# Keys of a pair of edge tiles turned into one PSUM bank, aggregates in three banks: a graph layer and an expert layer on Trainium2

## The chip, the cores and the metric

The kernel runs on one core of a Trainium2 chip. The metric is the device time of one execution in microseconds; for the kernel before it is the median of three runs. A profile of one further execution goes with it. The engines are called PE (TensorE, the matmuls; PEld are its weight loads), DVE (VectorE), ACT (ScalarE), POOL or GpSimd, and SP (SyncE, which issues DMAs here).

## What is computed

The input is a graph of 3125 nodes with 256 features, 50,000 edges (source, target, type), and weights. There are three message-passing layers, a small perceptron on their result, and a layer of 8 experts of which each node uses two. The change lies in the edge part of the message passing, which is, cut to what matters:

```
Q = (h @ Wq.T + bq).reshape(-1, H, DH)          # H = 4 heads, DH = 64
K = (h @ Wk.T + bk).reshape(-1, H, DH)
V = (h @ Wv.T + bv).reshape(-1, H, DH)
scores = einsum('ehd,egd->ehg', Q[src], K[tgt]) / sqrt(DH)   # per edge, head against head
attn = softmax(scores, axis=-1)
msg = einsum('ehg,egd->ehd', attn, V[tgt]).reshape(-1, HID)
msg = msg + Ee[et]
return segment_sum(msg @ Wo.T + bo, src, num_segments=n_nodes)
```

All of it is in float32. The three layers are followed by `adjustment = relu(hidden @ W1.T + b1) @ W2.T + b2`, and the expert layer takes the top two of 8 experts by a softmax over `x @ Wr + br`.

## The kernel before

The program is written engine by engine, with semaphores set and awaited by hand. It first sorts the edges by source: the nodes are cut into windows of 16 nodes (W), and each tile of 128 edges holds edges of one window only. That gives 294 pairs of edge tiles per layer. A layer is then an edge phase (the function `e_phase`, present once on each engine) and a node phase (`uq_phase`, at the end `uf_phase`). The change touches the edge phase alone. There are three edge phases of 294 pairs, 882 pairs in all.

An edge phase goes through the pairs in 24 full turns of 12 pairs and a last one of 6; the turns between the first and the last are a hardware loop, so a turn's code is written out for 12 pairs. Per pair:

- GpSimd gathers the rows of keys and values (2 KB each) of the targets, one indirect DMA of 128 rows per tile, two per pair (line 574). They go into `kv`, a ring of 24 tiles, so the gathers for a pair start when the aggregates of the pair 12 places earlier are done (the wait on `agg_done` ahead of them).
- PE turns the keys, four transposes of 128 x 128 per pair (`key`, line 1544), into PSUM bank 3 or 4 by turns, and ACT copies that bank to `kt_s` (`keys`, line 1307), which has two buffers.
- ACT also lays the queries of the two windows into a block-diagonal operand (`queries`, lines 1302 and 1303).
- PE multiplies: two masks (`mask`, line 1548) set to a large negative number what doesn't belong to an edge's node, and eight instructions add the scores (`scores`, line 1574), in bank 0, 1 or 2.
- DVE takes the maximum over the 16 nodes, which picks an edge's own scores (`best`, line 829). Every four pairs it does the softmax with ACT's exponential, and per pair it spreads the weights over the window's nodes (`spread`, line 858).
- PE forms the aggregates, the weighted sum of values by node, with eight instructions (`aggregate`, line 1584), in bank 6 or 7 by turns. ACT copies them to `stage`, a ring of three, in two instructions (`sums_out`, line 1314), and DVE adds them to the window's sum (`add`, line 876).

The order of each engine's work is written out by hand. In step p, PE turns the keys of pair p + 1, with the masks of pair p between them (`keys_masks`), then makes the aggregates of pair p - 6 (LAG is 6), then the scores of pair p. ACT copies the keys of p, lays the queries of p + 1, and copies the sums of p - 7. DVE takes the maximum of p, spreads the weights of p - 4, and adds the sums of p - 7.

PE's waits in a step are these: before the keys and masks, for the maximum of pair p - 3 (its score bank is then free) and for the gathers of pair p + 1; before the aggregates, for the spread weights of p - 6 and for the staged sums of p - 8 (the aggregates' bank is then free, `staged` counts them and begins at 8); before the scores, for ACT's copy of the keys of p (`kT_ready`). Bank 5 holds DVE's small softmax results in an edge phase. The semaphores count on over turns and layers; `at[p]` is the count that is reached with pair p of the turn. Before the first layer's loop the counts of some semaphores are raised, so that the first waits pass.

Of the kernel before, what the change touches and what calls it, by code (L numbers as in the profile page):

```python
# [22 lines left out]
P = 128  # L23
N, D, H, DH, E, L = 3125, 256, 4, 64, 50000, 3
# [17 lines left out]
UB = 4  # L42
TURN = 6
EB = -(-(E + -(-N // W) * (P - 1)) // (P * UB))
EP = 2 * EB
# [4 lines left out]
PAIRS = TILES // 2  # L50
HT = TILES // 2
LASTP = 2 * LASTB
HALVES = 2 * NTURN - 1
LAG = 6
# [32 lines left out]
def build(nc, A, out):  # L87
    ctx = ExitStack()
    with ctx:
# [17 lines left out]
        ident = sb("ident", [P, P])  # L107
# [16 lines left out]
        kv = arena[:, 0:n_kv].rearrange("p (b u n) -> p b u n", b=TURN, u=UB)  # L124
# [33 lines left out]
        kt_s = sb("kt_s", [P, 2, 2, KC, P])  # L158
# [156 lines left out]
        bank = [ctx.enter_context(nc.psum_tensor(f"bank{i}", [P, 512], F32)) for i in range(8)]  # L315
# [16 lines left out]
        S = namedtuple("Semaphores", names)(*[sem(n) for n in names])  # L332
# [44 lines left out]

        def u_bank(l, n):
            return bank[n % (4 if l < L - 1 else 3)]

        block = ctx.enter_context(nc.Block())

# [843 lines left out]
        def _(act):  # L1226

            for c in range(NCH):
                b = c % 2
# [64 lines left out]
            def e_phase(l):  # L1294
                def indices(i, h):
                    act.activation(gidx[:, h, :], rec[:, ds(i * TILES + h * HT, HT)], ACT.Copy).then_inc(S.idx_ready, 1)

                def queries(p):
                    for u in range(2):
                        w = act.snap(areg[2 * p + u], min_val=0, max_val=NW - 1)  # L1300
                        q = qt[:, ds(w, 1), :].squeeze(1)
                        act.activation(qbd[0:DH, p % 4, u, 0:64], q, ACT.Copy)  # L1302
                        act.activation(qbd[DH:P, p % 4, u, 64:128], q, ACT.Copy)  # L1303

                def keys(p, at):
                    act.wait_ge(S.kT_done, at[p])
                    act.activation(kt_s[:, p % 2], bank[3 + p % 2][:, :].rearrange("p (u c n) -> p u c n", u=2, n=P),  # L1307
                                   ACT.Copy).then_inc(S.kT_ready, 1)

                def sums_out(p, done, added):  # L1310
                    act.wait_ge(S.agg_done, done)
                    act.wait_ge(S.chain_b, added)
                    for r in range(2):
                        ins = act.activation(  # L1314
                            stage[r * DH:(r + 1) * DH, p % 3].rearrange("p u (h s) -> p u h s", h=H),
                            bank[6 + p % 2][r * DH:(r + 1) * DH, 0:2 * P].rearrange("p (u g s h) -> p g u h s", u=2, g=2, h=H)[:, r],
                            ACT.Copy)
                    ins.then_inc(S.staged, 1)

                def exps(n, ready):  # L1320
                    act.wait_ge(S.exp_in, ready)
                    act.activation(ex[:, 0:2 * n], sx[:, 0:2 * n], ACT.Exp).then_inc(S.exp_out, 1)

                def turn(i, first, last, before_last=False):
                    pairs = LASTP if last else PAIRS
                    at = [act.snap(l * EP + i * PAIRS + p + 1) for p in range(2 * PAIRS - AL)]
                    before = None if first else act.snap(l * EP + i * PAIRS)
                    for p in range(pairs):
                        keys(p, at)
                        if p + 1 < pairs:  # L1330
                            queries(p + 1)
                        elif not last:
                            act.load(areg, wid[0:1, ds((i + 1) * TILES, TILES)])
                            queries(0)
                        if p >= AL or not first:
                            sums_out((p - AL) % PAIRS, at[p + PAIRS - AL], at[p - 1] if p else before)
                        if p % GP == 1 and (p > 1 or not first):
                            exps(GP, act.snap(l * EG + i * GT + p // GP))
                        if p == PAIRS // 2 - 1 and not last:
                            indices(i + 1, 0)  # L1340
                        if p == PAIRS - 1 and not before_last:
                            indices(i + 1, 1)

                for h in range(2):
                    indices(0, h)
                act.load(areg, wid[0:1, 0:TILES])
                queries(0)
                turn(0, True, False)
                with nc.scalar.Fori(1, NTURN - 2) as i:
                    turn(i, False, False)  # L1350
                turn(NTURN - 2, False, False, True)
                turn(NTURN - 1, False, True)
                exps(LASTP - GP * (GL - 1), act.snap(l * EG + EG))
                for p in range(AL):
                    sums_out((LASTP - AL + p) % PAIRS, act.snap(l * EP + EP + p + PAIRS - AL + 1), act.snap(l * EP + EP + p))
# [100 lines left out]
        def _(pe):  # L1456
# [83 lines left out]
            def e_phase(l):  # L1540
                def key(p, u, c):
                    t = 2 * p + u
                    o = u * D + c * P
                    return pe.transpose(bank[3 + p % 2][:, o:o + P], kv[:, t // UB, t % UB, c * P:(c + 1) * P], ident[:, :])  # L1544

                def mask(p, u):
                    m = 2 * (p % 4) + u
# [4 lines left out]
                def keys_masks(k, landed, p, at, here):  # L1552
                    if p is not None:
                        pe.wait_ge(S.score_read, at[p + 1])
                        if p % 4 == 0:
                            pe.wait_ge(oh_landed[p // 4], here[p // 4 // 2])
                    for u in range(2):
                        if k is not None:
                            pe.wait_ge(gathered[2 * k + u], landed)
                        for c in range(KC):  # L1560
                            if k is not None:
                                ins = key(k, u, c)
                            if u == 0 and p is not None:
                                mask(p, c)
                    if k is not None:
                        ins.then_inc(S.kT_done, 1)

                def scores(p, at):
                    bk = bank[p % 3]
                    pe.wait_ge(S.kT_ready, at[p])  # L1570
                    for u in range(2):
                        for c in range(KC):
                            o = u * D + c * P
                            ins = mm(bk[:, o:o + P], kt_s[:, p % 2, u, c, :], qbd[:, p % 4, u, :],  # L1574
                                     start=False, stop=(c == KC - 1), skip_group_check=True)
                    ins.then_inc(S.score_done, 1)

                def aggregate(p, ready):
                    pe.wait_ge(S.att_ready, ready)
                    pe.wait_ge(S.staged, ready)  # L1580
                    for t in (2 * p, 2 * p + 1):
                        b, u, o = t // UB, t % UB, t % 2 * P
                        for g in range(0, H, 2):
                            ins = mm(bank[6 + p % 2][:, o:o + P], kv[:, b, u, D + g * DH:D + (g + 2) * DH],  # L1584
                                     att[:, b % 2, u, :, g:g + 2, :].rearrange("p s g h -> p g s h"),
                                     start=(g == 0), stop=(g == H - 2), skip_group_check=True)
                    ins.then_inc(S.agg_done, 1)

                def turn(i, first, last):
                    pairs = LASTP if last else PAIRS  # L1590
                    at = [pe.snap(l * EP + i * PAIRS + p + 1) for p in range(pairs + 1)]
                    here = [pe.snap((l * (NTURN - h) + i + 1) * 16) for h in range(2)]
                    ahead = pe.snap((l * NTURN + i + 2) * 16)
                    for p in range(pairs):
                        if p + 1 < pairs:
                            keys_masks(p + 1, here[(p + 1) * 2 // PAIRS], p, at, here)
                        elif not last:
                            keys_masks(0, ahead, p, at, here)
                        else:
                            keys_masks(None, None, p, at, here)  # L1600
                        if p >= LAG or not first:
                            aggregate((p - LAG) % PAIRS, at[p])
                        scores(p, at)

                keys_masks(0, pe.snap((l * NTURN + 1) * 16), None, None, None)
                turn(0, True, False)
# [1 line left out]
                    turn(i, False, False)  # L1608
                turn(NTURN - 1, False, True)
                for p in range(LAG):  # L1610
                    aggregate((LASTP - LAG + p) % PAIRS, pe.snap(l * EP + EP + p + 1))

            def update(l, n, ring):
                dst, at = u_bank(l, n), l * NT + n + 1
# [291 lines left out]
```

## Time and profile before

| | |
|---|---|
| three runs, us | 4463.02, 4485.4, 4497.68 |
| median, us | 4485.4 |
| the profiled execution, us | 4478.05 |
| its span, us | 4476.2 |
| mean granted PE clock over the span | 0.918 |
| PE, PEld, DVE, ACT, POOL busy, share of the span | 81%, 71%, 55%, 60%, 53% |

The span is what the trace covers: from the first instruction to the last. Times in a trace are microseconds from its start, those marked ns apart. Busy time doesn't count register, branch, semaphore and DMA-issuing instructions. PE's matmuls are pipelined and their ends are modelled, so that a matmul's bar reaches past the start of the next. Where an engine sat idle, the trace names what ended the wait, as far as the semaphores show it; "remote" is a releaser that it can't name and "issue" is no wait that it can see. A part of the matmul records can be missing.

### The profile page before, as it was taken

Reading aid. Unit: us, or ns where it says so; the run is one execution under the profiler, and the core shown is the slowest. Engines: PE = TensorE matmul, PEld = TensorE weight load, DVE = VectorE, ACT = ScalarE, POOL = GpSimd, SP = SyncE. Lnnn points to the kernel's source line nnn. Section 1 sums busy time; section 2 is a strip of 40 time slices with the busy share of each in tenths; the row PEclk is TensorE's granted clock in tenths of the full one; section 3 lists DMA queues with packets and bytes.
Section 4 is the critical chain, followed back from the end, with each engine's and each line's share of the span. In section 5 each row is a group of like instructions: output and inputs, shape, how many; then the busy total and the mean of one; then the engine's idle time right before and its main releaser. Section 6 shows DMA issues by size and latency. Waiting matters only on the chain.

```text
span 4476.2 us, 90208 instructions
## 1 busy us (share of the span) xinstructions
PE 3636.6 (81%) x26290; PEld 3156.6 (71%) x26291; DVE 2448.8 (55%) x6794; ACT 2699.9 (60%) x8426; POOL 2356.7 (53%) x2552
## 2 busy tenths in 40 slices
PE   6777868887888887788878888878888888887999
PEld 2333547787777775777777777577777777767998
DVE  6555635565656664566566566455566565682111
ACT  4666766666666655666666665566666666543443
POOL 3555324555555565555555555545555555563444
PEclk9777888999999999999999999889999999898999
DMA  2000154555555534555555553445555555445665
GB/s 66 0 0 0 40 198 136 157 165 161 161 162 160 164 116 159 145 165 163 163 165 162 160 162 110 153 141 160 160 164 164 160 158 159 142 158 181 179 186 126
DMA packets 264904, 630.76 MB, mean 141 GB/s; under 512 B 56095, under 2 KB 128726, under 8 KB 256471
## 3 DMA queue, kind: packets, MB, share of 16 engines
q0 software_dynamic: 161376, 477.59, 38.4%
q1 hardware_dynamic: 103431, 152.05, 10.1%
q8 instruction: 40, 0.66, 0.1%
q14 instruction: 57, 0.47, 0.0%
HBM read 577.72 MB, written 52.04 MB: 141 GB/s over the span
## 4 chain that ended last, share of the span: by engine, by line
PE 56%; DVE 14%; issue 12%; another core or an unknown queue 10%; ACT 5%; DVEq 2%; DMA 1%; ACTq 0%; POOL 0%; SPq 0%; POOLq 0%
PE bank L1584 13%; PE bank L1574 12%; PE bank L1777 5%; PE bank L1544 4%; PE bank L1789 4%; DVE att L858 4%; PE bank L1530 3%; PE bank L1548 2%; PE bank L1482 2%; DVE arena L876 2%; DVE sc L829 2%; PE bank L1496 2%; PE bank L1490 2%; PE bank L1524 2%
## 5 line engine op out<-in xcount | busy, mean ns | idle before, releaser
L574 POOL DMA_INDIRECT arena<-kv_d,gidx x1764 | 1672.3, 948 | 1492.4 <-PE bank L1584 514.9
L1584 PE MATMUL bank<-att,arena 128*128 128x128 f32 x7056 | 1023.5, 291 | 494.4 <-DVE att L858 391.2
L1584 PEld LDWEIGHTS bank<-att,arena 128*128 128x128 f32 x7056 | 909.3, 202 | 583.0 <-DVE att L858 468.3
L829 DVE TENSOR_REDUCE sc<-bank 128x32 f32<-128x512 f32 x882 | 606.5, 688 | 948.9 <-remote 513.6
L1574 PE MATMUL bank<-qbd,kt_s 128*128 128x128 f32 x7056 | 1014.8, 290 | 67.0 <-issue 34.2
L1307 ACT ACTIVATE kt_s<-bank 128x512 f32<-128x512 f32 x882 | 526.6, 597 | 870.1 <-PE bank L1544 552.9
L1574 PEld LDWEIGHTS bank<-qbd,kt_s 128*128 128x128 f32 x7056 | 933.3, 205 | 78.4 <-issue 40.4
L1544 PE MATMUL bank<-ident,arena 128*128 128x128 f32 x3528 | 766.0, 283 | 51.1 <-issue 25.7
L858 DVE TENSOR_TENSOR att<-bank,oh 128x512 f32<-128x512 f32 x882 | 602.1, 683 | 26.4 <-PE bank L1584 0.4
L1314 ACT ACTIVATE stage<-bank 64x128 f32<-64x128 f32 x1764 | 478.4, 271 | 164.5 <-PE bank L1584 118.6
L1544 PEld LDWEIGHTS bank<-ident,arena 128*128 128x128 f32 x3528 | 493.7, 148 | 82.3 <-issue 54.0
L876 DVE TENSOR_TENSOR arena<-stage,arena 128x64 f32 x1764 | 400.6, 227 | 196.1 <-issue 94.5
L1302 ACT ACTIVATE qbd<-arena 64x64 f32 x1764 | 441.5, 250 | 50.7 <-issue 40.4
L1303 ACT ACTIVATE qbd<-arena 64x64 f32 x1764 | 449.2, 255 | 20.5
L1548 PE MATMUL bank<-maskc,oh 128*128 128x256 bf16 x1764 | 453.5, 282 | 4.2 <-issue 4.2
L558 POOL DMA_INDIRECT rec_d<-arena x241 | 245.1, 1017 | 257.7 <-DVE arena L770 186.4
L756 DVE CUSTOM_DVE_ANT_0 arena<-bank,arena 128x200 f32<-128x200 f32 x391 | 138.8, 364 | 193.7 <-PE bank L1496 102.7
L1214 DVE TENSOR_TENSOR arena<-bank,arena 128x256 f32<-128x256 f32 x56 | 23.8, 425 | 356.6 <-PE bank L1789 356.6
L1234 ACT ACTIVATE arena<-arena 128x592 bf16<-128x592 f32 x150 | 105.2, 776 | 181.5 <-DVE arena L773 177.3
L1490 PE MATMUL bank<-arena 128*128 128x200 bf16 x391 | 114.5, 305 | 118.4 <-DVE rank L756 77.3
L1777 PE MATMUL bank<-xT,arena 128*128 128x128 f32 x1792 | 210.5, 276 | 0.1
L1777 PEld LDWEIGHTS bank<-xT,arena 128*128 128x128 f32 x1792 | 205.7, 193 | 0.5 <-ACT xT L1437 0.5
(246 smaller groups left out, 4211.8 us busy)
## 6 DMA issues: line engine op xcount, KB each, us to landing
arena<-in_pack SPq DMA_DIRECT2D x56, 1030.0 KB
arena<-kv_d,gidx POOLq DMA_INDIRECT x1764
oh<-oh_d SPq DMA_DIRECT2D x222, 64.0 KB
kv_d<-arena SPq DMA_DIRECT2D x50, 256.0 KB, 2.0
xin<-hid_d SPq DMA_DIRECT2D x75, 128.0 KB
arena<-in_w SPq DMA_DIRECT2D x8, 1024.0 KB, 8.3
kv_d<-arena SPq DMA_DIRECT2D x5, 1280.0 KB, 5.1
hid_d<-arena SPq DMA_DIRECT2D x50, 128.0 KB, 2.0
```

Of the source, the lines that this page charges most:

```text
L574: pool.indirect_dma_start(kv[:, t // UB, t % UB, :], None, kv_d, bass.IndirectOffsetOnAxis(gidx[:, h, t - h * HT:t - h * HT + 1], 0),).the ...
L829: dve.tensor_reduce(sc[:, 2 * m:2 * m + 2], bank[q % 3][:, :].rearrange("p (t g s h) -> p t g h s", t=2, g=H, s=W), AX.X, ALU.max).then_in ...
L858: dve.tensor_tensor(att[:, b, u:u + 2].rearrange("p t s g h -> p t s (g h)"), at_s[:, 2 * m:2 * m + 2].rearrange("p t g h -> p t (g h)").u ...
L876: dve.tensor_tensor(a, stage[:, p % 3, u, :], a, ALU.add).then_inc(S.chain_a if u == 0 else S.chain_b, 1)
L1303: act.activation(qbd[DH:P, p % 4, u, 64:128], q, ACT.Copy)
L1307: act.activation(kt_s[:, p % 2], bank[3 + p % 2][:, :].rearrange("p (u c n) -> p u c n", u=2, n=P), ACT.Copy).then_inc(S.kT_ready, 1)
L1314: ins = act.activation(stage[r * DH:(r + 1) * DH, p % 3].rearrange("p u (h s) -> p u h s", h=H), bank[6 + p % 2][r * DH:(r + 1) * DH, 0:2 ...
L1544: return pe.transpose(bank[3 + p % 2][:, o:o + P], kv[:, t // UB, t % UB, c * P:(c + 1) * P], ident[:, :])
L1548: mm(bank[p % 3][:, u * D:(u + 1) * D], oh[:, p // 4, 1, :], maskc[:, m:m + 1, :].to_broadcast([P, H, DH]), start=(u == 0), stop=False, sk ...
L1574: ins = mm(bk[:, o:o + P], kt_s[:, p % 2, u, c, :], qbd[:, p % 4, u, :], start=False, stop=(c == KC - 1), skip_group_check=True)
L1584: ins = mm(bank[6 + p % 2][:, o:o + P], kv[:, b, u, D + g * DH:D + (g + 2) * DH], att[:, b % 2, u, :, g:g + 2, :].rearrange("p s g h -> p ...
L1777: ins = mm(bank[1 + 2 * (p % 2) + h // 4][:, (h % 4) * P:(h % 4 + 1) * P], w1s[:, p, c * HID + h * P:c * HID + (h + 1) * P], xT[:, p % 2, ...
```

## The change

The keys of a pair are turned into bank 3 alone, and the aggregates go round three banks, 4, 6 and 7. So PE must have ACT's copy of the keys of pair p before it turns those of pair p + 1, and the wait on `kT_ready` moves from the scores to the head of the step; only the last step of a phase, which turns no keys, keeps it at the scores. The aggregates of pair p - 6 then need the staged sums of p - 9 in place of p - 8, so their wait on `staged` is for one less; a register `before` holds that count for the first pair of a turn.

```diff
+        def sum_bank(p):
+            return bank[(4, 6, 7)[p % 3]]
...
-                    act.activation(kt_s[:, p % 2], bank[3 + p % 2][:, :].rearrange("p (u c n) -> p u c n", u=2, n=P),
+                    act.activation(kt_s[:, p % 2], bank[3][:, :].rearrange("p (u c n) -> p u c n", u=2, n=P),
...
-                            bank[6 + p % 2][r * DH:(r + 1) * DH, 0:2 * P].rearrange("p (u g s h) -> p g u h s", u=2, g=2, h=H)[:, r],
+                            sum_bank(p)[r * DH:(r + 1) * DH, 0:2 * P].rearrange("p (u g s h) -> p g u h s", u=2, g=2, h=H)[:, r],
...
-                    return pe.transpose(bank[3 + p % 2][:, o:o + P], kv[:, t // UB, t % UB, c * P:(c + 1) * P], ident[:, :])
+                    return pe.transpose(bank[3][:, o:o + P], kv[:, t // UB, t % UB, c * P:(c + 1) * P], ident[:, :])
...
                         if p % 4 == 0:
                             pe.wait_ge(oh_landed[p // 4], here[p // 4 // 2])
+                    if k is not None and p is not None:
+                        pe.wait_ge(S.kT_ready, at[p])
...
-                def scores(p, at):
+                def scores(p, at, last):
                     bk = bank[p % 3]
-                    pe.wait_ge(S.kT_ready, at[p])
+                    if last:
+                        pe.wait_ge(S.kT_ready, at[p])
...
-                def aggregate(p, ready):
+                def aggregate(p, ready, emptied):
                     pe.wait_ge(S.att_ready, ready)
-                    pe.wait_ge(S.staged, ready)
+                    pe.wait_ge(S.staged, emptied)
...
-                            ins = mm(bank[6 + p % 2][:, o:o + P], kv[:, b, u, D + g * DH:D + (g + 2) * DH],
+                            ins = mm(sum_bank(p)[:, o:o + P], kv[:, b, u, D + g * DH:D + (g + 2) * DH],
...
+                    before = None if first else pe.snap(l * EP + i * PAIRS)
...
-                            aggregate((p - LAG) % PAIRS, at[p])
-                        scores(p, at)
+                            aggregate((p - LAG) % PAIRS, at[p], at[p - 1] if p else before)
+                        scores(p, at, last and p + 1 == pairs)
...
-                    aggregate((LASTP - LAG + p) % PAIRS, pe.snap(l * EP + EP + p + 1))
+                    aggregate((LASTP - LAG + p) % PAIRS, pe.snap(l * EP + EP + p + 1), pe.snap(l * EP + EP + p))
```

## Rows read from the trace of the kernel before

**Rows 1.** Table by stretch; busy us of PE, PEld, DVE, ACT, POOL; PEclk

```profile
645.00:1653.00 1008.00, 810.12 (x6466) 767.01 (x6467) 603.11 (x1542) 633.61 (x2174) 563.66 (x604) 0.93 0.55 159
...
sum 3022.00, PE 2429.77 PEld 2301.01 DVE 1784.51 ACT 1900.87 POOL 1690.48; mean PE 809.92 PEld 767.00 DVE 594.84 ACT 633.62 POOL 563.49
```

**Rows 2.** Groups by line; columns: busy us, mean ns, idle before, releasers

```profile
L574 POOL DMA_INDIRECT arena<-kv_d,gidx x1764 | 1672.3, 948 | 1492.4 <-PE bank L1584 514.9 <-issue 488.9 <-remote 352.6
...
L1584 PE MATMUL bank<-att,arena 128*128 128x128 f32 x7056 | 1023.5, 291 | 494.4 <-DVE att L858 391.2 <-issue 91.8 <-ACT stage L1314 9.3
...
L1574 PE MATMUL bank<-qbd,kt_s 128*128 128x128 f32 x7056 | 1014.8, 290 | 67.0 <-issue 34.2 <-ACT kt_s L1307 32.0
...
L829 DVE TENSOR_REDUCE sc<-bank 128x32 f32<-128x512 f32 x882 | 606.5, 688 | 948.9 <-remote 513.6 <-PE bank L1574 404.9 <-issue 28.9
...
L1307 ACT ACTIVATE kt_s<-bank 128x512 f32<-128x512 f32 x882 | 526.6, 597 | 870.1 <-PE bank L1544 552.9 <-remote 259.8 <-issue 45.4
```

**Rows 3.** Waits: us in total, times, longest

```profile
PE bank L1574 <- ACT kt_s L1307: 32.0, 14, 17.1
```

**Rows 4.** Timeline of GpSimd: start, duration, gather, idle before

```profile
948.54 0.94 POOL L574 DMA_INDIRECT arena<-kv_d,gidx  x1 [1.85 <-PE bank L1584]
...
954.79 0.95 POOL L574 DMA_INDIRECT arena<-kv_d,gidx  x1 [0.30 <-issue]
...
958.16 0.94 POOL L574 DMA_INDIRECT arena<-kv_d,gidx  x1 [2.43 <-remote]
...
961.46 0.94 POOL L574 DMA_INDIRECT arena<-kv_d,gidx  x1 [1.10 <-PE bank L1584]
...
968.22 0.95 POOL L574 DMA_INDIRECT arena<-kv_d,gidx  x1 [1.39 <-PE bank L1584]
...
974.73 0.95 POOL L574 DMA_INDIRECT arena<-kv_d,gidx  x1 [1.82 <-PE bank L1584]
```

**Rows 5.** Timeline of a held stretch

```profile
951.55 0.38 PE L1544 MATMUL bank<-ident,arena 128*128 128x128 f32 x2
...
953.91 1.06 PE L1574 MATMUL bank<-qbd,kt_s 128*128 128x128 f32 x8
...
954.69 0.14 PEld L1544 LDWEIGHTS bank<-ident,arena 128*128 128x128 f32 x1
...
957.25 0.69 DVE L829 TENSOR_REDUCE sc<-bank 128x32 f32<-128x512 f32 x1 [3.86 <-remote]
...
957.32 0.60 ACT L1307 ACTIVATE kt_s<-bank 128x512 f32<-128x512 f32 x1 [4.39 <-PE bank L1544]
...
958.59 2.08 PE L1584 MATMUL bank<-att,arena 128*128 128x128 f32 x8 [1.86 <-DVE att L858]
```

**Rows 6.** Timeline of quiet steps

```profile
945.00 0.60 ACT L1307 ACTIVATE kt_s<-bank 128x512 f32<-128x512 f32 x1
...
945.31 0.14 PEld L1544 LDWEIGHTS bank<-ident,arena 128*128 128x128 f32 x1
...
945.97 0.97 PEld L1584 LDWEIGHTS bank<-att,arena 128*128 128x128 f32 x8
...
961.96 0.15 PEld L1544 LDWEIGHTS bank<-ident,arena 128*128 128x128 f32 x1
...
962.50 0.38 PE L1544 MATMUL bank<-ident,arena 128*128 128x128 f32 x2
...
962.62 0.97 PEld L1584 LDWEIGHTS bank<-att,arena 128*128 128x128 f32 x8
...
962.92 0.60 ACT L1307 ACTIVATE kt_s<-bank 128x512 f32<-128x512 f32 x1 [1.37 <-PE bank L1544]
...
963.51 0.97 PEld L1574 LDWEIGHTS bank<-qbd,kt_s 128*128 128x128 f32 x8
...
964.40 0.14 PEld L1544 LDWEIGHTS bank<-ident,arena 128*128 128x128 f32 x1
```

**Rows 7.** Table by stretch, after the held stretch

```profile
958.50:961.90 3.40, 3.31 (x15) 3.31 (x16) 1.95 (x7) 2.93 (x11) 2.00 (x3) 0.51 0.46 118
```

## The prediction

> **What bounds the kernel now.** I looked first at the three edge phases in the table by stretch [rows 1]. They are 3022 of the 4476.2 us of the span, 3022/882 = 3.43 us for each of the 882 pairs of edge tiles, and no engine is full in them: PE is busy about 81% of them, GpSimd 56%, the others 59 to 63%. So I went to the groups by line [rows 2], to the waits [rows 3] and to the timeline. A step of PE has three parts: 4 turned keys with 2 masks between them, 8 aggregate instructions, 8 score instructions. Where nothing holds it, the first weight loads of the parts stand at 961.96, 962.62, 963.51 and, for the next step, 964.40 [rows 6]: 0.66 + 0.89 + 0.89 = 2.44 us. The other 1.0 us per pair is waiting, and the last columns of the groups say on whom: aggregates on DVE's spread weights, 391 us; gathers of GpSimd on aggregates, 515 us; DVE's maximum on something unnamed, 514 us; ACT's copy of the keys on PE, 553 us. PE waits for that copy (line 1307) only 32.0 us, 14 times [rows 3], and its aggregates wait for a staged sum (line 1314) 9.3 us in all.
>
> The timeline shows where these waits come from. PE's last turned key of a pair ends at 951.93 (951.55 + 0.38), but ACT, idle, starts to copy it at 957.32, and DVE starts its maximum at 957.25 [rows 5]. In the quiet case the same distance is 0.04 us (962.50 + 0.38, copy at 962.92) [rows 6]. Between the two GpSimd sends six gathers without a break, 948.54 to 955.74, and both engines wake 1.5 us after the last [rows 4]. This repeats: PE's signals are held from about 2 us into a row of gathers until 1.1 to 1.5 us after it, then come all at once. I have no cause for it from the trace; I take it as the beat of the phase. A row of gathers is two per pair, and GpSimd starts a pair when its aggregates are signalled. From start to next start, rows of 2 gathers last 3.62 us on average (155 of them; here 961.46 - 958.16 = 3.30), rows of 4 6.60 us (227; here 974.73 - 968.22 = 6.51), rows of 6 9.58 us (63; here 9.62) [rows 4]. Per pair that is 3.62, 3.30 and 3.19 us.
>
> **The change, part by part.** (1) The aggregates' wait becomes weaker: three banks (4, 6, 7), so they need the staged sum of three pairs ago, not two. All that it can give back is what the old wait costs: 9.3 us [rows 2]. Behind those waits the spread weights are late next, so I take 0, between 0 and -9.3.
>
> (2) The scores' wait for the copied keys goes; in its place PE waits for the same copy one part-step earlier, before it turns the next pair's keys into the one bank. Nothing is added to any engine's work, and no DMA moves. What is queued behind the new wait is PE's whole step: 4 turned keys, 2 masks, 8 aggregates and 8 scores; for them wait ACT's next copy, DVE's maximum and, through the aggregates, GpSimd's gathers. Before, PE could do turned keys and aggregates (0.66 + 0.89 us) before it needed the copy.
>
> How late the copy would be is read from the timeline, step by step: end of the copy of a pair, plus 0.05 us, less the start of the next pair's turned keys. It is late in 491 of 879 steps, 754 us in sum. One of each kind: at 945.31 PE turns keys while the copy runs until 945.60 and so comes 0.34 us late, and the aggregates follow at once at 945.97 [rows 6], so all of it would push PE. At 954.69 PE turns keys while the copy comes at 957.32 to 957.92 [rows 5]: 3.28 us late, but the aggregates of this step wait for DVE until 958.59. With the change the turned keys start at 957.97, end their part at 958.63, and the aggregates start 0.04 us later than now. Of the 754 us, 477 are covered within their own step by such a wait (326 steps); 204 us fall on 165 steps whose aggregates follow at once, 73 us are left over in the others: 277 us push PE.
>
> These 277 us are not yet time of the kernel. PE is not the bound for long: a hold of 2 to 3 pairs follows, and at its end PE waits for DVE again. 37% of the lateness survives its own step (277/754). If the same share survives each of the next steps up to the next hold, about two (445 rows of 2, 4 and 6 gathers for 882 pairs), 277 x 0.37 x 0.37 = 38 us are left at its end. Ends: 0, if the next wait takes all, and +277, if PE's delay is never made good. I take 38, nearer to the lower end, since now the aggregates wait 391 us for DVE, and for the copy PE waits 32.0 us.
>
> The Trainium skill, page Perfetto Trace Analysis, section Matmuls, says that independent matmul groups should go round different PSUM banks, so that the evacuation of one overlaps the next group; for the turned keys the change does the opposite. By that rule each copy (0.597 us, 882 of them [rows 2]) would lie bare: 527 us more. The trace doesn't bear out the full rule: one round of keys in a quiet stretch, turning and copying, is 0.66 + 0.27 + 0.04 + 0.60 + 0.05 = 1.62 us, inside PE's 2.44 us, since aggregates and scores go to other banks meanwhile.
>
> (3) The rest: one more register per turn, the tail of six aggregates with the looser wait, waits only in the last step for the last copy. Costed at 0: PE's waits of 1.0 us per pair hide it.
>
> Sum: 0 + 38 + 0. The profiled execution took 4478.05 us, with 1.9 us around its span; that makes 4516. The median of the runs shown is 4485.4, 7 us above the profiled one, so I place the forecast at 4485.4 + 38 = 4524 us, 0.9% slower.
>
> **The rivals.** *Slower by clearly over 1%: the hold bites twice.* After a hold PE needs a fresh copy before it can turn the next keys, and if the signal of those keys then falls into the next hold, PE stops one pair earlier than now. The 63 rows of 6 gathers break into 4 and 2: 6.60 + 3.62 - 9.58 = 0.64 us each, 40 us. Beside it PE stands idle longer in one piece: in the held case from 954.97, the end of the scores, to 957.97, 3.0 us, in place of 1.86 before the aggregates, and what follows such a pause runs at 0.51 of the clock [rows 7], the lower of its two levels (1.2 GHz): the 8 aggregates took 2.08 us there [rows 5], in a quiet step 0.89 + 0.27 = 1.16 [rows 6]. With only the first cover of the delay, 277 x 0.37 = 102 us, this makes +142: 4627 us. For it speaks that 491 steps are late; against it that the aggregates stopped at nearly the same moment already. It decides where rows of 6 become rare and rows of 2 more than 155. By the rule of the page above, the trend would be this way.
>
> *Faster: the beat evens out.* The wait keeps PE from running into the hold in single pairs, and single rows merge: if two thirds of the 155 rows of 2 join in pairs, 52 times 2 x 3.62 - 6.60 = 0.64 us, 33 us, with the 9.3 us of the looser wait and no delay left: -42, 4443 us. For it speaks that the mix of rows is set by small shifts; against it that the change only adds a wait where waits matter.
>
> *The change does nothing:* aggregates are what PE waits for in every hold, delays are all made good: 0, 4485 us. For it: the 0.04 us of the held case above. It shares the outcome "within 1%" with the forecast.
>
> **How the numbers follow.** Forecast (+10 to +75) 0.40, nothing (within 10 us) 0.17, clearly slower 0.28, faster 0.15. A measurement of this kernel can tell about 1%, 45 us, from no change. Of the forecast's share 0.11 lie above 45 us, of the faster rival's 0.03 inside it: slower 0.39, same 0.49, faster 0.12. The range from 4455 to 4610 leaves out the far part of the faster rival (0.08) and the upper end of the slower one (0.12).
>
> **What would show it right or wrong.** Right: the waits before PE's turned keys name ACT's copy, over a hundred times, and the aggregates' wait for DVE's spread weights goes down from 391 us in return; before the scores PE waits for no copy; no aggregate waits for a staged sum; PE's work, GpSimd's 948 ns a gather and the 1454 us outside the phases are unchanged; the mean row of gathers keeps its length. Wrong: if the edge phases take over 1040 us each, with rows of 2 gathers more than 200 and a granted clock under 0.90 (the slower rival); if they take under 1000 us with fewer rows of 2 (the faster one); or if they change while PE waits for the copy less than 50 us, which would mean that the path is not the one that I describe.

## The result, and the profile after

The median after is 4517.9 us against 4485.4 before (nine runs of each). The ratio is 1.0069 [1.0049, 1.0089]: 0.7% slower, about 31 us. 38 us were forecast. Over the runs shown the two ranges don't overlap (4463.0 to 4497.7 before, 4499.5 to 4532.7 after). The profiled execution of after has a span of 4519.8 us and a mean clock of 0.930 (before 4476.2 us and 0.918).

The table by stretch of the kernel after, with the three edge phases as windows (columns as in [rows 1]):

```profile
651.00:1672.00 1021.00, 801.36 (x6471) 749.64 (x6472) 605.48 (x1539) 634.81 (x2172) 565.60 (x604) 0.95 0.55 157
...
sum 3060.00, PE 2400.22 PEld 2256.41 DVE 1791.24 ACT 1904.52 POOL 1697.11; mean PE 800.07 PEld 752.14 DVE 597.08 ACT 634.84 POOL 565.70
```

The windows are 38 us longer than in [rows 1]. From the first turned key to the last aggregate of each phase it is 3022.9 us before and 3056.1 after: +33.2. The other 10.4 us of the two profiled spans lie outside the phases, 6.6 of them before the first; the change touches no code there, and the medians of the runs differ by only 32.5. Note PE's column: its busy time went *down*, from 2429.8 to 2400.2 us, at a granted clock of 0.95 in place of 0.93. So all of the loss, and 30 us more, is PE standing idle: in the windows 592 us before, 660 after.

The groups by line of the kernel after, which answer to [rows 2]:

```profile
L577 POOL DMA_INDIRECT arena<-kv_d,gidx x1764 | 1676.5, 950 | 1521.9 <-issue 523.0 <-PE bank L1590 497.0 <-remote 364.6
...
L1590 PE MATMUL bank<-att,arena 128*128 128x128 f32 x7056 | 993.8, 286 | 90.5 <-DVE att L861 63.0 <-issue 25.2 <-ACT stage L1317 1.9
...
L1580 PE MATMUL bank<-qbd,kt_s 128*128 128x128 f32 x7056 | 974.1, 283 | 1.1 <-issue 1.0
...
L1547 PE MATMUL bank<-ident,arena 128*128 128x128 f32 x3528 | 764.7, 284 | 588.0 <-issue 280.9 <-DVE sc L832 163.0 <-ACT kt_s L1310 119.4
...
L832 DVE TENSOR_REDUCE sc<-bank 128x32 f32<-128x512 f32 x882 | 607.5, 689 | 985.6 <-remote 557.8 <-PE bank L1580 401.7 <-issue 25.0
...
L1310 ACT ACTIVATE kt_s<-bank 128x512 f32<-128x512 f32 x882 | 526.8, 597 | 932.3 <-remote 773.4 <-PE bank L1547 112.7 <-issue 34.7
```

Read the idle column of PE's three lines together. The aggregates waited 494.4 us and now 90.5; the scores 67.0 and now 1.1; the turned keys 51.1 and now 588.0. The wait has moved to the head of the step, and it grew by 67 us on the way (612.5 to 679.6). The work is the same: ACT's copy takes 597 ns as before, a gather 950 ns (948), the maximum 689 (688).

Among the waits of the kernel after (us in total, times, longest) ACT's copy now stands before the turned keys:

```profile
PE bank L1547 <- ACT kt_s L1310: 119.4, 89, 3.2
```

That row names only a part of them. "Issue" has 280.9 us of the same column, and the timeline of the kernel after shows what hides in it:

```profile
968.29 0.94 POOL L577 DMA_INDIRECT arena<-kv_d,gidx  x1 [0.30 <-issue]
...
968.37 1.06 PE L1580 MATMUL bank<-qbd,kt_s 128*128 128x128 f32 x8
...
970.35 0.60 ACT L1310 ACTIVATE kt_s<-bank 128x512 f32<-128x512 f32 x1 [2.84 <-remote]
...
971.01 0.14 PEld L1547 LDWEIGHTS bank<-ident,arena 128*128 128x128 f32 x1 [1.78 <-issue]
...
971.19 0.95 POOL L577 DMA_INDIRECT arena<-kv_d,gidx  x1 [1.96 <-remote]
```

GpSimd's row of gathers ends at 969.23. ACT, idle for 2.84 us, starts its copy at 970.35, that is 1.1 us after it, and ends at 970.95. PE's next turned keys start at 971.01, 0.06 us behind the copy, and yet the row calls the 1.78 us before them "issue". The new wait stands in a semaphore instruction of its own, ahead of the matmul's own waits, and the profile doesn't always name what ended it.

### The profile page after: what moved, and what is told of

Its sections match the earlier page's. It is cut to its first block, busy times and chain, and to the rows that moved or that the text cites. A ratio compares the mean times of both kernels' runs of the same rounds, so it can differ in the third digit from the quotient of the medians.

```text
span 4519.8 us, 90476 instructions
## 1 busy us (share of the span) xinstructions
PE 3594.3 (80%) x26290; PEld 3108.6 (69%) x26291; DVE 2455.7 (54%) x6794; ACT 2706.2 (60%) x8426; POOL 2363.3 (52%) x2552
## 4 chain that ended last, share of the span: by engine, by line
PE 42%; another core or an unknown queue 16%; ACT 15%; issue 14%; DVE 9%; ACTq 2%; DVEq 1%; DMA 1%; POOL 0%; SPq 0%; POOLq 0%
PE bank L1590 7%; PE bank L1580 6%; PE bank L1784 4%; ACT stage L1317 4%; ACT qbd L1305 4%; PE bank L1796 4%; PE bank L1547 4%; ACT qbd L1306 4%; PE bank L1533 3%; PE bank L1485 2%; DVE att L861 2%; DVE sc L832 2%; PE bank L1527 2%; PE bank L1551 1%
## 5 line engine op out<-in xcount | busy, mean ns | idle before, releaser
L1547 PE MATMUL bank<-ident,arena 128*128 128x128 f32 x3528 | 764.7, 284 | 588.0 <-issue 280.9
L1590 PE MATMUL bank<-att,arena 128*128 128x128 f32 x7056 | 993.8, 286 | 90.5 <-DVE att L861 63.0
L1590 PEld LDWEIGHTS bank<-att,arena 128*128 128x128 f32 x7056 | 895.6, 199 | 136.4 <-DVE att L861 94.2
L1580 PE MATMUL bank<-qbd,kt_s 128*128 128x128 f32 x7056 | 974.1, 283 | 1.1 <-issue 1.0
L1547 PEld LDWEIGHTS bank<-ident,arena 128*128 128x128 f32 x3528 | 482.2, 144 | 686.1 <-issue 463.8
L1580 PEld LDWEIGHTS bank<-qbd,kt_s 128*128 128x128 f32 x7056 | 903.5, 200 | 1.8 <-issue 1.8
```

The source lines that it names most:

```text
L1547: return pe.transpose(bank[3][:, o:o + P], kv[:, t // UB, t % UB, c * P:(c + 1) * P], ident[:, :])
L1590: ins = mm(sum_bank(p)[:, o:o + P], kv[:, b, u, D + g * DH:D + (g + 2) * DH], att[:, b % 2, u, :, g:g + 2, :].rearrange("p s g h -> p g s h"),
```

## The experiments

All are compared with the kernel before on the same chip, by ratio with its 95% interval; chips differ by up to 2% between calls (the kernel before had medians of 4467.99, 4487.66 and 4401.94 us in them).

**One part alone: the wait, with the banks as they were.**

```diff
# before, and nothing else changed
+                    if k is not None and p is not None:
+                        pe.wait_ge(S.kT_ready, at[p])
...
-                    pe.wait_ge(S.kT_ready, at[p])
+                    if last:
+                        pe.wait_ge(S.kT_ready, at[p])
```

> The kernel before with the wait on the copied keys moved ahead of the next pair's turned keys, and nothing else: banks stay as before (keys in two, sums in two). Theory (the earlier wait alone costs the 33 us): about +33 us, 4510 to 4525; rows of 6 gathers fall from 63 to about 10 and rows of 2 rise from 155 to over 300. Rival (the bank itself matters, PE writing where ACT has just read, or the looser wait on the sums changes the order of things): clearly less than +33 us, near 4485.

Measured: 4513.69 us, ratio 1.0096 [1.0074, 1.0118]; edge phases 3068.5 us in the profiled execution, which was the slowest of the six (4532.52 us). The mix of rows of gathers changed as expected: 405 rows of 2 and 14 of 6. Its groups by line, PE's turned keys:

```profile
L1544 PE MATMUL bank<-ident,arena 128*128 128x128 f32 x3528 | 765.7, 284 | 564.6 <-DVE sc L829 213.1 <-issue 212.9 <-ACT kt_s L1307 111.5
```

564.6 us of idle time before the turned keys, nearly what the whole change shows (588.0). So the place of the wait makes the loss, and no cost of its own can be seen for the single bank. The whole change is 0.27 points better than the wait alone, which the looser wait of the aggregates (9.3 us, 0.2%) could give, but the intervals overlap.

**The other part alone: three banks for the sums, two for the keys.** This needs bank 5, so the small softmax results `at_s`, which lie there, moved from PSUM to SBUF; the second run makes that move alone.

```diff
# e2_sums_three
-        at_s = bank[5][:, 0:2 * GP * H * H].rearrange("p (t g h) -> p t g h", g=H, h=H)
+        at_s = sb("at_small", [P, 2 * GP, H, H])
...
+        def sum_bank(p):
+            return bank[5 + p % 3]
...
-                            aggregate((p - LAG) % PAIRS, at[p])
+                            aggregate((p - LAG) % PAIRS, at[p], at[p - 1] if p else before)
# e3_small_sbuf: the first two lines alone
```

> Keys in two banks as before, sums in three (5, 6, 7) with their looser wait; DVE's small softmax results, which had bank 5, lie in SBUF. Theory (the third bank for the sums is worth nothing, the old wait cost 9.3 us): within 10 us of before, give or take what DVE gains or loses on 222 small operations, 4470 to 4495. Rival (the looser wait is worth something which the earlier wait on the keys hid): 4450 or less.

> The kernel before with DVE's small softmax results in SBUF in place of bank 5, and nothing else (keys in two banks, sums in two, old waits). It splits the 41 us that the run with three banks for the sums gained. Theory (the move to SBUF did it, since the mean gather went from 0.948 to 1.060 us there, so GpSimd's rows of gathers change when DVE reads both inputs from SBUF): 4425 to 4440 on a chip where before takes 4468 to 4485, mean gather about 1.06 us, rows of 8 and more gathers. Rival (the looser wait on the sums, with three banks, did it): within 10 us of before, rows of gathers as before (63 of 6, none of 8).

Measured: 4421.85 us, ratio 0.9908 [0.9877, 0.9939], and 4435.84 us, ratio 0.9887 [0.9848, 0.9926]. The first run fell into its rival's range, but not for its rival's reason: the move to SBUF alone is as fast, so the third bank adds nothing that can be measured (the two ran on different chips, each against the kernel before there). The move was to be a mere aid and turned out to be worth 1.1%. The groups by line of the second run, GpSimd's gathers:

```profile
L574 POOL DMA_INDIRECT arena<-kv_d,gidx x1764 | 1853.4, 1051 | 1276.8 <-issue 518.4 <-PE bank L1584 394.2 <-remote 226.4
```

A gather takes 1051 ns in the mean in place of 948 [rows 2]: the median is still 0.95 us, but one in ten takes 1.42 us or more. GpSimd is thus busy 181 us longer, and yet it stands idle 216 us less (1276.8 against 1492.4). The trace shows which gathers are long. With the move, the spread of the weights on DVE (line 858, 882 operations of 0.69 us) reads both its inputs from SBUF. All 361 gathers that take over 1.2 us began while such a spread ran, and the 847 that met none take 0.95 us; in the kernel before 887 gathers meet a spread, and none of them takes over 1.2 us.

**The same with the wait on top.** The kernel after, with the same line moved.

```diff
# after
-        at_s = bank[5][:, 0:2 * GP * H * H].rearrange("p (t g h) -> p t g h", g=H, h=H)
+        at_s = sb("at_small", [P, 2 * GP, H, H])
```

> The changed kernel with DVE's small softmax results in SBUF in place of bank 5. That move made the kernel before 1.1% faster, with holds that begin later. Theory (the earlier wait costs through the holds): with weaker holds it costs no more than before, so 4435 to 4470 us. Rival (the two effects are apart and add): the same 1.1% off 4518, 4468 us; if the wait costs more than that where rows are long, as with forced rows of six, 4480 us or more.

Measured: 4420.56 us, ratio 1.0034 [1.0012, 1.0056]. Against the same move without the change that is 1.0034/0.9887 = +1.5%: the change costs more here, not less, and the theory written down for this run is wrong. The quotient joins two chips, so it holds only as far as the ratio of the move carries over from one to the other.

**Are the data of the gathers what holds PE's signals?** Both kernels with gathers of 256 B a row in place of 2 KB; the count of gathers is the same.

```diff
-                                kv[:, t // UB, t % UB, :], None, kv_d, bass.IndirectOffsetOnAxis(...), 0),
+                                kv[:, t // UB, t % UB, 0:64], None, kv_d.rearrange("r (k n) -> (r k) n", k=8), bass.IndirectOffsetOnAxis(...), 0),
```

> The kernel before, but each gather brings 64 floats per row (256 B) in place of 512 (2 KB), from other rows; count of gathers and of rows is the same. PE works on what lies in the buffer, so the result isn't the reference's. Theory D (PE's signals are held by the data of the gathers on its way): the holds vanish, PE, DVE and ACT run at 2.5 to 2.7 us per pair, 3850 to 3950 us in all. Theory G (they are held by GpSimd's work on the descriptors itself): holds of 1.1 to 1.5 us after each row of gathers stay, 4400 us or more.

> The changed kernel with the same small gathers (256 B per row, so not the reference's result). If the holds are what makes the earlier wait dear: where they vanish, it costs nothing, within 5 us of the small-gather version of the kernel before, since a round of keys is 1.6 us in a step of 2.44. If the holds stay, again about +33 us. Rival (the wait costs by ACT's own order, holds or not): +20 us or more even without holds.

Measured: 4479.94 us, ratio 0.999 [0.9951, 1.0029], and 4541.84 us, ratio 1.0145 [1.0112, 1.0178]. With an eighth of the bytes the kernel takes the same time. Its groups by line, DVE's maximum:

```profile
L829 DVE TENSOR_REDUCE sc<-bank 128x32 f32<-128x512 f32 x882 | 606.6, 688 | 961.5 <-PE bank L1574 511.5 <-remote 429.4 <-issue 20.2
```

It is idle 961.5 us, as before (948.9), and its signals from PE are mostly prompt in the first 2 us of a row of gathers and then seldom. The DMA queue of the gathers took 7.5% of the DMA engines' time in place of 38.4%. So the hold doesn't come from the bytes that are moved. GpSimd's own work on a gather and the count of rows are the same in both kernels (946 and 948 ns a gather), and this run doesn't tell them apart. The new wait costs 1.0145/0.999 = +1.55% here, about 69 us, more than the 33 that were expected.

**No gathers in the edge phases.** Both kernels without the gathers of the edge phases and the waits for their landing; the rest of the work stands.

```diff
-                            pool.indirect_dma_start(...).then_inc(gathered[t], 16)
+                            pass
...
-                            pe.wait_ge(gathered[2 * k + u], landed)
```

> The kernel before with the 1764 gathers of the edge phases and the waits for them left out; PE works on what lies in the buffer, so the result isn't the reference's. Theory (GpSimd's gathers hold PE's signals): no holds, PE's step of 2.44 us sets the pace with a little above, 2.5 to 2.65 us per pair, 3680 to 3830 us in all. Rival (the holds have another source): 3.3 us per pair remain, 4400 us.

> The changed kernel with the same gathers left out. Theory (the earlier wait costs because a held signal of the turned keys now stops PE one part-step earlier): without holds a round of keys, 1.62 us, fits a step of 2.44, so within 10 us of the version of before without gathers. Rival (it costs through ACT's own order of work, where ACT reaches the copy late): +20 us or more.

Measured: 3663.15 us, ratio 0.8319 [0.8291, 0.8348], and 3661.57 us, ratio 0.8308 [0.8281, 0.8335]. The table by stretch and a group of the kernel before without gathers:

```profile
645.00:1407.00 762.00, 748.56 (x6488) 722.55 (x6487) 600.73 (x1591) 640.36 (x2169) 38.57 (x68) 0.99 0.03 10
```

```profile
L827 DVE TENSOR_REDUCE sc<-bank 128x32 f32<-128x512 f32 x882 | 607.0, 688 | 211.4 <-PE bank L1570 208.8
```

PE is busy for 748.56 of 762 us at a clock of 0.99; the "remote" wait of DVE, 513.6 us before, is gone. A pair takes 2250.6/882 = 2.55 us, near the 2.44 us of a quiet step, in place of 3.43. This run takes away GpSimd's work and the waits for landing along with the holds, so its 17% are the most that the holds can be worth and not their price. And the kernel after without gathers:

```profile
L1545 PE MATMUL bank<-ident,arena 128*128 128x128 f32 x3528 | 724.4, 273 | 19.0 <-DMA oh<-oh_d 6.5 <-DVE sc L830 5.3 <-ACT kt_s L1308 5.3
```

The wait for ACT's copy costs 5.3 us in 882 steps, and the whole kernel is 1.6 us faster than without the change, which is nothing. Without gathers, and so without holds, the change is free.

**A hold of the same length in every third pair.** In both kernels GpSimd waits for the aggregates of three pairs and then sends its six gathers in one row. This sets the row by hand: it adds waits of its own, so only the two runs are compared with each other.

```diff
-                        hold(pool, S.agg_done, after[p])
+                        if p % 3 == 0:
+                            hold(pool, S.agg_done, after[p + 2])
```

> The kernel before, but GpSimd waits for the aggregates of three pairs and then sends their six gathers in one row, so nearly all rows have 6 or more. Theory (the mix of rows sets the pace, 3.19 us per pair in rows of 6 against 3.36 on average): edge phases 882 x 3.19 = 2814 us at best in place of 3023, so 4300 to 4420 us. Rival (rows only mirror how far PE got; forced rows don't make PE faster, and the held stretch gets longer): 4470 us or more.

> The changed kernel with the same rows of six gathers. Theory (the earlier wait costs by breaking rows of 6 into rows of 2): with the rows forced, it costs less than 15 us against the forced version of the kernel before. Rival (it costs because PE can do fewer aggregates in a hold, whatever the rows): more than 33 us, up to 60.

Measured: 4898.18 us, ratio 1.0927 [1.0874, 1.098], and 5343.73 us, ratio 1.1911 [1.1851, 1.1971]. The forced rows are slower, not faster as I had thought. Between the two kernels lie 445.5 us, where under 15 were expected and the rival had said 33 to 60. Rows of six gathers (279 in each trace) last 11.49 us from start to start in the one, 13.10 in the other: 1.61 us each, and 279 x 1.61 = 449. That is a difference of two means. No single row need show it: in the first kernel half of the rows last 10.5 us or less and the others about 12 or 14, in the second half last 13.4 us or more. Nor is all of it waiting. The tables by stretch of the two kernels, in this order:

```profile
sum 3433.00, PE 2553.89 PEld 2368.13 DVE 1779.01 ACT 1901.43 POOL 1685.77; mean PE 851.30 PEld 789.38 DVE 593.00 ACT 633.81 POOL 561.92
...
sum 3879.00, PE 2847.53 PEld 2709.96 DVE 1794.60 ACT 1898.39 POOL 1689.23; mean PE 949.18 PEld 903.32 DVE 598.20 ACT 632.80 POOL 563.08
```

Of the 446 us by which the edge phases grew, 294 are PE doing the same work for longer, at a granted clock of 0.80 in place of 0.92, and 152 are PE standing idle. The timeline of the kernel before with forced rows:

```profile
1041.48 0.14 PEld L1545 LDWEIGHTS bank<-ident,arena 128*128 128x128 f32 x1
...
1042.50 0.94 POOL L575 DMA_INDIRECT arena<-kv_d,gidx  x1 [0.30 <-issue]
1042.60 0.98 PEld L1585 LDWEIGHTS bank<-att,arena 128*128 128x128 f32 x8 [0.43 <-issue]
...
1044.85 0.60 ACT L1308 ACTIVATE kt_s<-bank 128x512 f32<-128x512 f32 x1 [5.19 <-remote]
...
1045.95 0.94 POOL L575 DMA_INDIRECT arena<-kv_d,gidx  x1 [2.51 <-PE bank L1585]
```

And of the kernel after with forced rows:

```profile
1098.89 0.94 POOL L578 DMA_INDIRECT arena<-kv_d,gidx  x1 [0.30 <-issue]
...
1101.24 0.60 ACT L1311 ACTIVATE kt_s<-bank 128x512 f32<-128x512 f32 x1 [5.68 <-remote]
1101.91 0.14 PEld L1548 LDWEIGHTS bank<-ident,arena 128*128 128x128 f32 x1 [4.45 <-issue]
...
1102.96 1.83 PEld L1591 LDWEIGHTS bank<-att,arena 128*128 128x128 f32 x8
...
1105.88 0.94 POOL L578 DMA_INDIRECT arena<-kv_d,gidx  x1 [6.04 <-PE bank L1591]
```

In the first, PE turns the next keys and makes the next aggregates inside the hold, at 1041.48 and 1042.60, before the copy that comes at 1044.85; the next row of gathers starts 2.51 us after the last. In the second, keys and aggregates stand behind the copy, and the row starts 6.04 us after the last. (The pair shows the ends. GpSimd waits for aggregates 282 times in each kernel, 1257.5 us in the first, 4.5 us each, and 1706.5 us in the second, 6.1 us each.) Here, too, the aggregates take 1.83 us behind a pause of 4.45 us, and the mean clock of the run falls from 0.910 to 0.826: this is what the slower rival feared.

**Would it help to put the masks ahead of the wait?** The two masks of a step don't write the keys' bank; in this kernel they come before the wait.

```diff
# after
+                    if p is not None:
+                        for c in range(2):
+                            mask(p, c)
                     if k is not None and p is not None:
                         pe.wait_ge(S.kT_ready, at[p])
...
-                            if u == 0 and p is not None:
-                                mask(p, c)
```

> The changed kernel with the two masks of a step ahead of the wait on the copied keys, so that PE has them to do while it waits; same work, other order. Theory of lateness (what counts is how long PE stands before the keys): the wait is met by 0.22 us later in a step that PE enters free, so a part of the cost comes back, +15 to +28 us against before in place of +33. Rival (what counts is only which signals get out before a hold, and the turned keys are signalled later still): +30 us or more.

Measured: 4520.12 us, ratio 1.0087 [1.0059, 1.0115]; nothing that can be measured is regained. Its groups by line, the aggregates and the turned keys:

```profile
L1591 PE MATMUL bank<-att,arena 128*128 128x128 f32 x7056 | 1009.0, 288 | 169.6 <-DVE att L861 114.4 <-issue 52.9 <-ACT stage L1317 1.9
...
L1547 PE MATMUL bank<-ident,arena 128*128 128x128 f32 x3528 | 572.6, 286 | 467.3 <-ACT kt_s L1310 361.1 <-issue 88.0 <-DMA arena<-kv_d,gidx 15.9
```

The waits before the keys are shorter by 121 us (467.3 against 588.0) and no time is won. The greater part of them has only moved on: the aggregates now wait 169.6 us in place of 90.5. Two more things can be read here. With nothing else in the way the profile names ACT's copy as their releaser, 361.1 us, which bears out what lay under "issue" before. And its rows of gathers are 154 of 2, 287 of 4 and 22 of 6, not the 374, 195 and 10 of the kernel after: as many of 2 as in the kernel before (155), but fewer of 6 (63 there), and the same loss.

**A pause for the signals.** The kernel before, where GpSimd writes a scratch tile after each pair's gathers and waits for it.

```diff
+                        pool.memset(idle[:, :], 0.0).then_inc(S.slot_ready, 1)
+                        pool.wait_ge(S.slot_ready, ...)
```

> The kernel before with a pause of GpSimd after each pair's two gathers: it clears 128 x 256 floats of a scratch tile (0.3 to 0.5 us) and waits for that. Theory (PE's signals get out when the row of gathers is broken, as they did where DVE made gathers 0.1 us longer on average): signals later than 2 us in a row get through, DVE's and ACT's unnamed waits shrink, 4400 us or less. Rival (the hold counts GpSimd's instructions or rows and a short pause doesn't open it): the pause only adds to each pair's time, 4500 us or more.

Measured: 4537.51 us, ratio 1.0298 [1.0272, 1.0323]. Its groups by line:

```profile
L1587 PE MATMUL bank<-att,arena 128*128 128x128 f32 x7056 | 941.7, 277 | 11.9 <-DVE att L861 10.4 <-ACT stage L1317 1.4
...
L1547 PE MATMUL bank<-ident,arena 128*128 128x128 f32 x3528 | 838.4, 292 | 686.9 <-DMA arena<-kv_d,gidx 667.6 <-ACT stage L1317 8.4 <-issue 2.8
...
L832 DVE TENSOR_REDUCE sc<-bank 128x32 f32<-128x512 f32 x882 | 609.7, 691 | 1058.5 <-PE bank L1577 1039.9 <-issue 16.0
...
L578 POOL MEMSET idle<- 128x256 f32 x882 | 288.8, 327 | 0.5
```

The holds are gone: DVE waits for nothing unnamed any more, 99% or more of PE's signals that ACT or DVE stood waiting for arrive within 0.3 us, at any place of a row, and the clock is 0.958. The gathers bring the same data as before, at nearly the same share of the DMA engines (0.53 in the first phase, 0.55 before), so it is their following one another without a break that holds the signals. The time isn't won, since the pause is too long. GpSimd now takes 3.44 us on average for two gathers and the pause (1.24 us from the second to the next first, in place of 0.30), and PE waits 667.6 us for keys to land. The half of the theory on the signals holds; that the time would follow doesn't. A shorter pause wasn't tried, nor was the length of the pause told apart from the instruction that fills it.

## Why the prediction was right, point by point

**The bound.** Right, and the hold itself is now shown: it is gone without gathers, where the kernel is 17% faster, and gone with a pause in each pair. The trace's record of semaphore updates shows it as well. In the held stretch [rows 5] updates of DVE and ACT arrive at 952.87 to 953.00, but none of PE's between 950.65 and 957.22; then five of PE's come within 0.34 us. How much of the 17% the holds make is not shown, since the kernel without gathers also leaves out GpSimd's 2 x (0.948 + 0.30) = 2.50 us a pair, and the kernel with the pause is no faster.

**Step 1, the looser wait of the aggregates, worth 0.** Right. Their wait for a staged sum went from 9.3 us to 1.9, and a third bank for the sums bought nothing beside the move that made room for it (0.9908 against 0.9887).

**Step 2, the earlier wait.** The size was right (38 us forecast, 31 to 33 measured), and so was its sign and place: the wait alone gives 1.0096. The aggregates' idle time went down as forecast (DVE's spread weights from 391.2 to 63.0 us), the scores wait for no copy, and in 426 of 879 steps the turned keys now start within 0.07 us of the copy's end, near the 491 that were counted late. The profile names the copy only 89 times, not over a hundred; the others carry another name, "issue" for the most part. But that the size came out is in part luck. The working read from the trace that 37% of the late time pushes PE, and then took the same share twice more for the steps that follow; no run shows that it is the same there. The count of late time can be made in the same way for each kernel that has no early wait, and set beside what the wait cost there (for `at_s` in SBUF the cost joins two chips):

| kernel | late steps of 879 | late, us | forecast by 38/754 of it, us | cost of the wait, us |
|---|---|---|---|---|
| without gathers | 16 | 10 | 1 | 0 |
| before | 491 | 754 | 38 | 31 |
| small gathers | 487 | 763 | 38 | 69 |
| `at_s` in SBUF | 604 | 921 | 46 | 66 |
| forced rows | 577 | 1263 | 64 | 445 |

Lateness that comes with the holds is the right thing to look at: without it there is no cost. But the same lateness cost 31 us in one kernel and 69 in another, and with forced rows the forecast would have been wrong by a factor of seven. A fixed price for each hold does no better: spread over the rows of four or more gathers the costs are 0.10, 0.25 and 0.25 us in the three middle kernels and 1.6 us with forced rows. That 1.6 us is near one round of keys, 1.62 us in the prediction, but as two thirds of it are PE's slower clock, the agreement shows nothing. What decides how much of a round stays bare remains open.

**The Trainium skill**, page Perfetto Trace Analysis, section Matmuls, wants independent matmul groups to go round different banks. The prediction's estimate by that rule was 527 us for the bare copies. The runs agree only in part: in the kernel without gathers a single bank costs nothing (0.8308 against 0.8319), because aggregates and scores fill the round, in this kernel it costs 31 us, and with forced rows 445.

**Step 3, the rest, 0.** Nothing speaks against it. Work that was to stay the same did: 950 ns a gather, and PE's busy time in the windows fell by 30 us at the higher granted clock.

**"The mean row of gathers keeps its length."** This step failed. Rows of 6 fell from 63 to 10 and rows of 2 rose from 155 to 374, the mark of the slower rival. By the mean durations in the trace before, rows of odd length included, the new mix would cost 84 us; but a row of 2 is now 3.45 us long, not 3.62, and 374 x 0.17 = 64 us of it come back. With the masks ahead there are as few rows of 2 as before and the loss is the same, and long rows by force are slow. So the number of rows of 2 doesn't set the cost.

**The slower rival.** Its second half, a longer pause and a colder clock, didn't come: 0.93 became 0.95 in the phases. It came only where all rows were long by force (0.910 to 0.826 over the whole run). **The faster rival** and **nothing** are excluded by the interval of the ratio.

**What stays open.** That gathers sent without a break hold PE's signals is shown; why they do is not. As the ends of matmuls are modelled, the trace also can't tell a late signal from a matmul that really ended late. Nor is it shown why a gather made longer by a spread on DVE loosens the hold, or how long a pause has to be.

## What to carry to other kernels

What a second bank is worth is read from the trace and not from a rule: here a single one is free as long as another group of matmuls fills the round, and costs up to 445 us where the round begins only after a stall. When a wait moves ahead of other work, find the longest stalls of the phase and ask what the engine did in them that it can't do now; that tells where the cost will be, but no simple count gave its size here. Look at the clock too, since a longer pause can cost more through slower work than through the waiting. And where an engine sits idle although its producer has long finished, test the signal's way before tuning the work: leaving out one stream of DMAs bounded the gain at 17% here, and one small tile moved to SBUF in the kernel before gave 1.1%, by its ratio the fastest version of these that does all the work.

## What the runs showed that was not expected

- GpSimd's indirect gathers, sent back to back, hold PE's semaphore signals to ACT and DVE: from about 2 us into a row until, mostly, 0.8 to 1.3 us after its end (the middle half of the held signals in the kernel before), with ACT idle for 5.68 us in the stretch shown. An eighth of the bytes changes nothing (0.999); with no gathers (0.8319), or a pause of about 1.2 us in each pair (1.0298), the hold is gone.
- With `at_s` in SBUF the mean gather rises from 948 to 1051 ns, and the hold gets weaker: of PE's signals that ACT or DVE stood waiting for, 23, 52 and 63% are prompt (within 0.3 us) in the third, fourth and fifth microsecond of a row, against 17, 8 and 0% before. Later than 2 us into a row 77% of 57 signals are prompt where a long gather had begun in the last 2.5 us, and 32% of 118 elsewhere. The kernel is 1.1% faster although its gathers are 11% slower.
- The Trainium skill, page SBUF — State Buffer, section Who interferes with whom, says that a DVE instruction with two inputs in SBUF contends with a GpSimd instruction that reads SBUF. The trace agrees: a gather reads its indices (`gidx`) from SBUF, and all 361 that take over 1.2 us began during a spread with both inputs there.
- More waiting can go with a higher clock. PE had 67 us more idle time in the windows, but in shorter pieces: its pauses over 2 us fell from 85 to 51. Its granted clock went from 0.93 to 0.95.
